# Two encoder-decoder layers and a rotary attention layer: the last layer's heads laid out in 64 rows by DMAs

## What is computed

```python
q = rope((x @ Wq).reshape(B, Sq, 16, 64)); k = rope((ctx @ Wk).reshape(B, Skv, 16, 64))
# rope: r1 = x1*cos - x2*sin, r2 = x2*cos + x1*sin, with x1 the even and x2 the odd columns of a head
scores = einsum('bqhd,bkhd->bhqk', q, k) / 8          # masked keys: -1e9
out = einsum('bhqk,bkhd->bqhd', softmax(scores), (ctx @ Wv).reshape(B, Skv, 16, 64))
y = layer_norm(x + out.reshape(B, Sq, 1024) @ Wo)
```

## Time and profile before

| | |
|---|---|
| median of 3 runs | 525.77 us (523.55 to 526.3) |
| the profiled execution | 527.22 us |
| its span, first to last instruction | 525.3 us |
| PE busy | 506.3 us, 96% |
| DVE, ACT, POOL busy | 436.8, 367.6, 295.5 us |
| mean granted TensorE clock | 0.992 |
| DMA, share of the 16 engines from the second tenth of the span on | 0 to 2 tenths |

### The profile page before, as it was taken

One profiled execution on the slowest core, in us unless ns is written; L12 is line 12 of the kernel. 1 busy time (PEld: TensorE's weight loads), 2 busy tenths in 40 slices (PEclk: granted clock), 3 DMA queues, 4 the chain that ended last, 5 costly groups with the idle time before them and its releaser, 6 DMA issues.

```text
span 525.3 us, 23789 instructions
## 1 busy us (share of the span) xinstructions
PE 506.3 (96%) x10336; PEld 470.6 (90%) x10336; DVE 436.8 (83%) x776; ACT 367.6 (70%) x1002; POOL 295.5 (56%) x581
## 2 busy tenths in 40 slices
PE   6989999999999999999999999999999999999986
PEld 6789999999999999999999998889999999999885
DVE  4898999977889877877878788999889888888873
ACT  5676675765876766767567686678687887888761
POOL 2553534534437445343536335888777887887825
PEclk9999999999999999999999999999999999999989
DMA  7910000000012010000000000000000000000000
GB/s 236 316 69 4 4 2 2 2 4 2 3 42 82 2 43 3 2 3 1 4 2 2 2 2 2 3 3 4 2 8 9 14 8 9 13 8 9 7 9 21
DMA packets 10838, 12.74 MB, mean 24 GB/s; under 512 B 752, under 2 KB 8432, under 8 KB 10736
## 3 DMA queue, kind: packets, MB, share of 16 engines
q1 hardware_dynamic: 10736, 11.24, 7.0%
HBM read 10.18 MB, written 1.05 MB: 21 GB/s over the span
## 4 chain that ended last, share of the span: by engine, by line
PE 78%; ACT 12%; DVE 4%; issue 2%; POOL 1%; DMA 1%; SPq 0%; POOLq 0%; DVEq 0%
PE ps_p L677 14%; PE ps_p L507 7%; PE ps_p L648 7%; PE ps_p L509 7%; PE ps_p L508 7%; ACT kT L762 6%; PE ps_a L562 5%; PE ps_a L584 5%; PE ps_p L637 4%; PE ps_a L544 4%; PE ps_p L639 4%; PE ps_p L638 4%; PE ps_p L584 4%; PE ps_p L698 2%; ACT probs L800 2%; PE ps_a L555 2%
## 5 line engine op out<-in xcount | busy, mean ns | idle before, releaser
L1179 POOL TENSOR_TENSOR small<-mv,epsilon 128x1 f32<-128x1 f32 x48 | 9.6, 199 | 170.1 <-DVE mv L936 170.1
L677 PE MATMUL ps_p<-wo,headsT 128*128 128x128 f32 x768 | 95.3, 278 | 2.0 <-DVE headsT L915 0.9
L677 PEld LDWEIGHTS ps_p<-wo,headsT 128*128 128x128 f32 x768 | 91.4, 193 | 5.2 <-issue 1.9
L907 DVE TENSOR_TENSOR turn<-ps_p,rope 128x1024 f32<-128x1024 f32 x64 | 76.0, 1221 | 11.6 <-PE ps_p L509 10.2
L754 ACT ACTIVATE vv<-ps_p 128x512 f32<-128x512 f32 x96 | 57.1, 619 | 27.3 <-PE ps_p L639 23.8
L507 PE MATMUL ps_p<-xT_hi,wq_hi 128*128 128x256 f32 x192 | 58.6, 305 | 1.1 <-issue 0.8
L790 ACT ACTIVATE probs<-ps_a,top 128x64 f32<-128x64 f32 x256 | 56.0, 353 | 4.4 <-DVE top L980 3.4
L1010 DVE TENSOR_REDUCE total<-probs 128x16 f32<-128x1024 f32 x48 | 58.2, 1212 | 0.2
L762 ACT ACTIVATE qT<-ps_p,columns 128x256 f32<-128x256 f32 x126 | 49.4, 494 | 10.1 <-PE ps_p L509 10.1
L508 PE MATMUL ps_p<-xT_lo,wq_hi 128*128 128x256 f32 x192 | 54.2, 282 | 0.0
L509 PE MATMUL ps_p<-xT_hi,wq_lo 128*128 128x256 f32 x192 | 54.1, 282 | 0.0
(11 more groups left out here) (143 smaller groups left out, 1429.2 us busy)
## 6 DMA issues: line engine op xcount, KB each, us to landing
out<-y_out SPq DMA_DIRECT2D x16, 64.0 KB, 2.8
X<-in_x SPq DMA_DIRECT2D x1, 768.0 KB, 7.6
across<-in_across SPq DMA_DIRECT2D x1, 704.0 KB, 9.5
wq_raw<-in_L_xattn_sa_wq SPq DMA_DIRECT2D x2, 256.0 KB, 2.9
wk_raw<-in_L_xattn_sa_wk SPq DMA_DIRECT2D x1, 512.0 KB, 5.9
wv_raw<-in_L_xattn_sa_wv SPq DMA_DIRECT2D x1, 512.0 KB, 8.2
wo<-in_L_xattn_sa_wo SPq DMA_DIRECT2D x1, 512.0 KB, 8.2
wo<-in_L_xattn_ca_wo SPq DMA_DIRECT2D x1, 512.0 KB, 8.7
```

The costliest lines, as they stand in the source:

```text
L677: last = mm(bank[:, 0:E], headsT[:, p, :, :].rearrange("r b q -> r (b q)"), wo[:, layer % 2, p, :], start=(p == 0), stop=(p == PAIRS - 1))
L907: ins = V.tensor_tensor(turn[:, j % 2, :, :].rearrange("d a (h b t) -> d a h b t", h=2, t=S), bank[:, None, :].broadcast_to([128, 2, 512]) ...
```

## The change

The weights of the last layer's queries and keys are put in another order of columns before the launch, so that a group of 128 rows holds the even or the odd columns of four heads. POOL no longer adds into `qT` and `kT` but into `w_raw[0]` (groups 0 and 1) and `w_raw[1]` (groups 2 and 3). When both groups of such a pair are there, SP issues 8 DMAs from SBUF to SBUF, each of 32 rows, two pieces of 1 KB a row, 64 KB, which put the even and the odd half of a head below each other in `qT` or `kT`: this is a move. There are four a chunk, 32 in all. A head then has 64 rows, and the last layer uses the scores, maxima and exponentials of the other layers, with two banks; `fold` and the split last addition go. PE waits, before the scores of an even unit, for all moves of its chunk. POOL waits, before it adds the first group of a pair, until the former move out of that buffer has landed. SP waits for the two additions, and for the scores of the chunk before last, which read the same half of `qT` and `kT`.

From step 36 on the keys come half a chunk ahead: step 36 has the four query groups and key groups 0 and 1; each odd step has key groups 2 and 3 of its chunk first and then 0 and 1 of the next chunk; step 45 has only groups 2 and 3. The number of groups over all steps stays. The rest of the diff renames `split_heads` to `scaled_queries` and takes out its branches.

```diff
@@ -64,6 +64,20 @@
+KEYS_AHEAD = 36
+def rotated_keys(u):
+    g = projected(u)
+    if u < KEYS_AHEAD:
+        return [(j, g) for j in range(4)] if u % 2 else []
+    if u % 2 == 0:
+        return [(0, g), (1, g)] if u == KEYS_AHEAD else []
+    return [(2, g), (3, g)] + ([(0, g + 1), (1, g + 1)] if g + 1 < N // 2 else [])
...
@@ -115,16 +129,17 @@
     project = []
-    if projected(u) is not None:
+    if rotary(u):
+        project = ([] if u % 2 else [("Qr", j, "D") for j in range(4)]) + [("Kr", j, "D") for j, _ in rotated_keys(u)]
+    elif projected(u) is not None:
         name = "K" if u % 2 else "Q"
-        for j in range(4):
-            project.append((name + "r", j, "D") if rotary(u) else (name, j, ("AAAD" if u == FIRST else "ADAD" if u < 0 else "AAAA")[j]))
+        project = [(name, j, ("AAAD" if u == FIRST else "ADAD" if u < 0 else "AAAA")[j]) for j in range(4)]
     next_in = [("T", 0, "AD")] if u % 2 and by_head(u + 1) else []
         into, inside, outof = ffn if ffn_chunk(u) is not None else ([], [], [])
-        return deferred + into + project[:2] + heads + project[2:] + values + inside + result + outof + probabilities + next_in
+        return deferred + into + project[:2] + heads + project[2:4] + values + project[4:] + inside + result + outof + probabilities + next_in
     if ffn_chunk(u) is not None:
...
@@ -200,12 +215,27 @@
-def rotations(name, j):
-    return (0, 1) if (name, j) == ("Kr", 3) else (1,)
-ROTATED = Tally(lambda u: [(n, j, v) for n, j, _ in fills(u) if n[1:] == "r" for v in rotations(n, j)])
+ROTATED = Tally(lambda u: [(n, j) for n, j, _ in fills(u) if n[1:] == "r"])
+def group_chunk(u, name, j):
+    return projected(u) if name == "Qr" else dict(rotated_keys(u))[j]
+MOVES = [(u, n, j // 2, group_chunk(u, n, j)) for u in range(FIRST, END) for n, j, _ in fills(u) if n[1:] == "r" and j % 2]
+def moves_ahead(u, name, place):
+    of = [m[:2] for m in MOVES if m[2] == place]
+    return of.index((u, name))
+def moves_for(g, place):
+    return max(k for k, m in enumerate(m for m in MOVES if m[2] == place) if m[3] == g) + 1
...
@@ -436,6 +466,11 @@
+        def apart(place):
+            return w_raw[place][:, :].rearrange("d (h j t) -> d h j t", h=2, j=2)
...
@@ -496,6 +531,17 @@
                     sp.dma_start(result[:, done % UNITS:done % UNITS + 1, :], y_out[:, v:v + 1, :]).then_inc(stored[v], 16)
+                for _, name, place, g in [m for m in MOVES if m[0] == u]:
+                    sp.wait_ge(rotated, ROTATED.at(u, name, 2 * place + 1))
+                    sp.wait_ge(scored, SCORED.at(2 * g - 3))
+                    to = (qT if name == "Qr" else kT)[:, g % 2, 4 * place:4 * place + 4, :]\
+                        .rearrange("r (j two) t -> r two j t", two=2)
+                    for i in range(4):
+                        for half in range(2):
+                            at = 64 * (i // 2) + 32 * half
+                            sp.dma_start(to[at:at + 32, i % 2, :, :], apart(place)[32 * i:32 * i + 32, half, :, :])\
+                              .then_inc(moved[place], 16)
             for v in range(2):
...
@@ -516,36 +562,12 @@
-                if layer == 2:
-                    pe.wait_ge(rotated, ROTATED.at(u - 1 - v, "Kr", 3, v))
+                if v == 0 and layer == 2:
+                    for place in range(2):
+                        pe.wait_ge(moved[place], MOVED * moves_for(u // 2, place))
                 elif v == 0:
                     out_of_bank(u - 1, "K", 3)
-                if layer == 2:
-                    if u == 2 * UNITS:
-                        pe.wait_ge(setup_dve, FOLD)
-                        pe.wait_ge(headed, HEADED.before(u))
-                    for i in range(4):
-                        for b in range(2):
-                            of = slice(32 * i, 32 * i + 32)
-                            m = mask[of, 1, u % UNITS, b:b + 1, :]
-                            mm(ps_a[64 * b:64 * b + 64, i ^ b, 0:256], fold[of, :], m.broadcast_to([32, 4, S]),
-                               start=True, stop=False, skip_group_check=True)
-                    for quad in range(H // 4):
-                        for half in range(2):
-                            for i in range(4):
-                                for b in range(2):
-                                    t = (2 * v + b) * S
-                                    of = slice(32 * i, 32 * i + 32)
-                                    last = mm(ps_a[64 * b:64 * b + 64, i ^ b, 64 * quad:64 * quad + 64],
-                                              qT[of, par, 2 * quad + half, t:t + S], kT[of, par, 2 * quad + half, t:t + S],
-                                              start=False, stop=half == 1, skip_group_check=True)
-                    last.then_inc(scored, 1)
-                    return
...
@@ -650,18 +672,20 @@
                     n_w = "QK".index(name[0])
-                    g = projected(u)
+                    g = group_chunk(u, name, j) if name[1:] == "r" else projected(u)
                     x = [s[:, :, 0:2 * S] for s in inputs_of(g)[n_w]]
                     if j == 0:
-                        pe.wait_ge(act_emptied, EMPTY_A.at(turn_in_step(g), "T", 0))
-                        pe.wait_ge(dve_emptied, EMPTY_D.at(turn_in_step(g), "T", 0))
+                        turning = turn_in_step(g - UNITS // CU if name == "Kr" else g)
+                        pe.wait_ge(act_emptied, EMPTY_A.at(turning, "T", 0))
+                        pe.wait_ge(dve_emptied, EMPTY_D.at(turning, "T", 0))
                         if g * CU % UNITS == 0:
-                        of = slice(256 * j + k, 256 * j + 256, 2) if name[1:] == "r" else slice(128 * (2 * j + k), 128 * (2 * j + k) + 128)
+                        of = slice(128 * (2 * j + k), 128 * (2 * j + k) + 128)
                         last = split_product(by_unit(bank[:, CT * k:CT * k + CT]),
...
@@ -879,10 +898,8 @@
-                    if j >= 2:
-                        dve.wait_ge(rotated, ROTATED.at(u, name, j - 2, 1))
-                    elif ROTATED.before(u):
-                        dve.wait_ge(rotated, ROTATED.at(u - 1, "Qr" if u % 2 else "Kr", j + 2, 1))
+                    if ROTATED.at(u, name, j) > 2:
+                        dve.wait_ge(rotated, ROTATED.at(u, name, j) - 2)
                 if name in ("T", "FT"):
...
@@ -1131,14 +1135,15 @@
             def rotate(u, groups):
-                for j in groups:
-                    name, to = ("Kr", kT) if u % 2 else ("Qr", qT)
+                for name, j in groups:
                     pool.wait_ge(dve_emptied, EMPTY_D.at(u, name, j))
-                    parts = rotations(name, j)
-                    for v in parts:
-                        of = slice(128 * v, 128 * v + 128) if len(parts) == 2 else slice(0, CT)
-                        G.tensor_tensor(to[:, projected(u) % 2, 2 * j:2 * j + 2, of], *[t[:, :, of] for t in turned(j)],
-                                        ALU.add).then_inc(rotated, 1)
+                    if j % 2 == 0:
+                        if moves_ahead(u, name, j // 2):
+                            pool.wait_ge(moved[j // 2], MOVED * moves_ahead(u, name, j // 2))
+                        else:
+                            pool.wait_ge(w_ready[j // 2], parts_ready(2, j // 2))
+                    G.tensor_tensor(apart(j // 2)[:, :, j % 2, :], *turned(j), ALU.add).then_inc(rotated, 1)
...
@@ -1297,6 +1303,10 @@
+    for n in "qk":
+        w = arrays["L1_xattn_W" + n].reshape(E, H // 4, 2, 2, D // 2, 2)
+        arrays["L1_xattn_W" + n] = np.ascontiguousarray(w.transpose(0, 1, 5, 3, 2, 4).reshape(E, H * D))
     aps = {name: nc.dram_tensor("in_" + name, v.shape, mybir.dt.from_np(v.dtype), kind="ExternalInput").ap()
```

More of the change, by code:

```diff
@@ L176, in vector_steps @@
         if name == "max":
-            steps += [("max", at)] + ([("eighth",)] if by_head(u) and not split_heads(u) and at else [])
+            steps += [("max", at)] + ([("eighth",)] if by_head(u) and not scaled_queries(u) and at else [])
         elif name == "sum":
-            steps += [("sum",), ("recip",)] + ([] if split_heads(u) else [("rinv",)])
+            steps += [("sum",), ("recip",)] + ([] if scaled_queries(u) else [("rinv",)])
         elif name == "fstat":
@@ L223, in vector_order @@
     before = [("norm", j, u - 1) for j in range(1 if rest_by_scalar(u - 1) else 2)] if by_head(u - 1) else []
-    maxima = [("max", 0)] + ([] if split_heads(u) else [("max", 1)])
+    maxima = [("max", 0)] + ([] if scaled_queries(u) else [("max", 1)])
     fgain = [("fgain", 0)] if gained(u) is not None else []
@@ L391, in build @@
         rotated = sem("rotated")
+        moved = [sem(f"moved{k}") for k in range(2)]
         stored = [sem(f"stored{v}") for v in range(2)]
@@ L775, in heads_out, with scale_of @@
                       .then_inc(headed, 1)
+            def scale_of(u):
+                return 1.0 if scaled_queries(u) else float(D) ** -0.5
             def exponentials(u, j):
```

(42 more changed lines are left out.)

24 lines of the change are left out of this document (9 added, 15 removed).

## The result

The changed kernel takes 602.86 us (median of 4 runs, 601.33 to 604.01), the kernel before 524.84 us beside it on the same chip: a ratio of 1.149 [1.145, 1.154], slower by 78 us. The sign of the forecast was right, its size was not: 561 us with a range of 537 to 580 was said. The profiled execution has a span of 599.9 us against 525.3.

What follows compares the result with a forecast made beforehand. The prediction took PE's work in the last layer as the bound. Terms of 10.1 + 6.8 + 18.8 + 0.3 = +36.0 us on the profiled 527.22 gave 563.2; with the median 1.45 lower it said 561 us, range 537 to 580.

Steps and rivals of the forecast that it cites:

- The failed step: SP's issues of a move: seven distances of 0.43 us, 3.0 in all, SP held 3.4 us, so it keeps up.
- the steady pair: Two steps from 38 to 46: 25.0 us instead of 20.29, +4.7 each, +18.8 for four pairs.
- M: Time of one move from POOL's last add to the data being there: 5.3 us, bounds 4.2 and 7.1.
- Steps 33 and 35: Odd steps before the order changes: keys' adds, then their move, make them later by 3.9 and 2.2 us.
- The ring of waits: Steps 36 to 46: POOL waits for buffer 1 until 17.0 us into a pair, DVE's turns for POOL, PE for turns.
- quick moves: Rival for all moves: 4.2 us each and the clock stays high, +10 us, 536 us; chance 0.17.
- The clock's eight times 1.2: PE's clock falls after each of eight waits at the even scores from 32 to 46, costing 1.2 us each.
- POOL's wait for the buffer: Steps 36 to 46: adds of Kr2 and Kr3 wait until the queries' move leaves buffer 1, at 17.0 us.
- The scores' gain: Last layer's scores with 64 rows: 1.17 us instead of 1.61, 0.44 less in 16 steps, 7.0 us in all.
- The rival that the gain does not exist: 64-row scores take 1.6 us, not 1.17: at most 7 us more; chance 0.03 with hidden moves, about 526.
- Slow moves: Rival for all moves: landing 3.6 us or more, 7.1 a move, full clock loss, 588 us; chance 0.13.
- Hidden moves: Rival from step 38 on: below 2.7 us a move nothing waits, the scores' gain shows, 518.8 us; chance 0.07.

Runs made afterwards that it cites:

- e3: The changed kernel with each move in 4 DMAs of 64 rows, 128 KB each, instead of 8 of 32 rows, same result: 543.91 us, 1.038.
- e6: The changed kernel with a separate tile for the keys' sums, still 8 DMAs a move: 591.15 us, 1.129.
- e1: The changed kernel with 64-row scores but no moves and keys never ahead, heads mixed: 519.55 us, 0.990 of the kernel before.
- e7: The changed kernel with extra unused PE products before the even scores' waits and some output projections, to hold the clock up: 603.8 us, 1.153.
- e4: The changed kernel with each move as one straight DMA of 512 KB, heads mixed: 526.51 us, 1.003 of the kernel before.
- e9: The changed kernel with 4 DMAs a move, keys half then a whole chunk ahead, and a separate tile for keys' sums, same result: 520.51 us, 0.9925.
- e11: e9 with 8 DMAs a move instead of 4, same result: 557.83 us, 1.065 of the kernel before.
- e10: The kernel before plus four trains of 8 DMAs of 64 KB on idle SP, from HBM or SBUF, 128 or 32 rows: 524.01 us in a single run.

## Why the prediction was wrong, step by step

**The failed step** is the term "I take 0.43 each, 3.0 us" with what was built on it: "occupies SP for 3.4. Two moves a step are 6.9 of 10 us, so SP keeps up". The distance of two issues came from loads out of HBM and single stores; from SBUF to SBUF it is 0.64 us, and up to 0.8 on average in a move that has a long issue. A move holds SP for 5.06 to 6.25 us. In the steady pair the four moves and two stores hold it for 22.7 us, where a pair had taken 20.29. One M comes to 7 times 0.64 + 2.0 + 0.1 = 6.6, inside its bounds of 4.2 to 7.1. The time that SP is held had been given no bounds. Below, the growth of the lateness at the scores (starts after, less those in the earlier trace rows and the 494.56 that the prediction gives).

| scores of | forecast | measured |
|---|---|---|
| 32 | +3.2 | 348.87 - 344.86 = +4.0 |
| 34 | +7.1 | 379.77 - 369.14 = +10.6 |
| 36 | +10.1 | 412.76 - 393.21 = +19.6 |
| 38 | +16.9 | 447.19 - 413.50 = +33.7 |
| 46 | +35.7 | 571.02 - 494.56 = +76.5 |
| end of the span | +36.0 | 599.9 - 525.3 = +74.6 |

**Steps 33 and 35.** The sum put the keys' last move behind the keys' adds alone. In the trace it stands behind three other moves in SP, and the adds themselves wait until the queries' move has left buffer 1. SP, POOL and PE of the changed kernel, steps 34 and 35, and the scores that follow:
```profile
388.86 5.06 SPq L543 DMA_DIRECT2D qT<-wq_raw  x8
394.01 5.98 SPq L543 DMA_DIRECT2D qT<-wk_raw  x8
400.04 0.58 SPq L533 DMA_DIRECT2D out<-y_out  x1
400.72 5.33 SPq L543 DMA_DIRECT2D kT<-wq_raw  x8
401.54 2.55 POOL L1146 TENSOR_TENSOR wk_raw<-turn 128x512 f32<-128x512 f32 x2 [1.73 <-DMA qT<-wk_raw]
406.15 5.07 SPq L543 DMA_DIRECT2D kT<-wk_raw  x8
...
412.76 0.64 PE L577 MATMUL ps_a<-mask,eye_bf 64*64 64x512 bf16 x4 [7.58 <-DMA kT<-wk_raw]
```
From 388.86 to 411.22 SP has no gap above 0.1 us. The adds end at 404.09, and their move waits 2.06 us more for SP. That is a neglected queue; by the starts of the adds in this trace it would not have shown with 3.4 us a move, an estimate of mine that no run tests.

**The steady pair.** Forecast 25.0, measured 30.83. The ring of waits was right: Q0 and Q1 ended at 8.6 in the pair (forecast 8.2). From there to buffer 1 being free it took 531.63 - 518.53 = 13.1 us (forecast 17.0 - 8.2 = 8.8), +4.3: the first move held SP for 5.9 in place of 3.5 with its wake-up (+2.4), and the second took 7.2 from its first issue to the free buffer in place of 5.3 (+1.9). From the end of the keys' adds to the scores it took 6.6 (forecast 5.3), +1.3. With +0.4 at the start that is 6.0, of 5.8 to be explained. Four such pairs grew by 123.83 - 81.06 = 42.8 us (forecast 18.8); that is 24.0 of the 38.6 us by which the span's growth was missed, another 16.8 had come by the scores of 38, and the end gave 2.2 back. e3, whose moves are about as long as "quick moves" had them (M near 4.1), measured 543.9, where that rival's sum said 536 with no clock loss. So the sum comes within 8 us when it is given its M. The clock's eight times 1.2 would bring it to 546, but in e3's trace the clock fell at only three of the eight scores and its mean was 0.990, so those 8 us are not explained by that.

**POOL's wait for the buffer** was foreseen (26 us in 6 waits), but its way back to PE was not counted as a stall of PE. e6 prices the sharing at 11 us.

**The scores' gain** was 0.44 a step and is 0.32: 5.1 in place of 7.0 us. The follower of the two rows was not the same. The rival that the gain does not exist falls by e1.

**The clock.** 1.2 us times eight stood in the sum. The clock did fall to 0.50 around the scores of all eight waits, as the trace before had shown once. In the steady pair it delays the turn of Q0 by 1.56 us against e7, and that turn is in the pair's chain, so the term was of the right kind and near in size. What it is worth in the whole kernel stays open: e7 held the clock up and took as long, for buffer 0 came free too late and SP's issues took longer. The Trainium skill (TensorE: Matmul & The Clock Gate, section HAM oscillation) says that the low clock comes back in each round of such a loop. The trace agrees, with 0.50 in each of the eight rounds; that its full price is then paid in each, 4 us more in the sum, no run here shows.

**The rivals.** "Slow moves" gave 588 and was nearest, but it made the landing slow (3.6) and left the issues fast; the landing was the term that I had nearly right. "Hidden moves" set 2.7 us as its point. e4 has about 2.9 + 0.1 = 3.0, and from 38 on its pairs take 19.74 us: next to that point the moves are hidden and the scores' gain shows, as the rival said, and only the steps before 38 bring the total back to 526.5. e9 moves the point itself by fetching earlier and is faster. Where the 78 us are: e9 against the change shows that three edits take them all away; by themselves, fewer issues are worth 59 (e3) and the buffer some 11 (e6), and with the buffer and the order mended, 8 issues against 4 still cost 37 (e11 against e9). Not tried: issuing part of the moves from another engine.

## What to carry to other kernels

Price a train of DMAs twice: once as a latency (distance of the issues times their number, and one landing) and once as time for which the queue's engine is held, and write that engine's instructions down in order before saying that it keeps up. Take the distance from issues with the same kinds of source and destination, and if no row has them, give the distance bounds that also go into the queue's sum. A slow clock behind a wait can lie in the chain and still give nothing back when it is mended, if a buffer or a queue comes right behind it (e7); look for that one before adding the clock's price.

## What the runs showed of the hardware that was not expected

- An issue on SP took 0.59 to 0.60 us from SBUF to SBUF and 0.42 to 0.43 from HBM, with the same bytes and rows (e10). More bytes did not make an issue longer: 64 KB 0.597, 128 KB 0.607, 512 KB in a single DMA 0.465. Why SBUF to SBUF is dearer is open. That the source lies in SBUF isn't enough, since a y_out store takes 0.33 when alone, and 0.58 right behind a train of moves.
- The queries' moves held SP for 5.81 and 5.63 us in the steady pair and the keys' for 5.06 each, with the same shapes. The difference is single long issues, 14 of the 256, of up to 1.71 us. All 14 overlap in time with a packet of 16 KB that the trace calls "instruction", and no such packet that runs while a move is being issued meets normal issues only. In the ten kernels with moves, 115 of the 116 issues of over 0.8 us overlap with such a packet. That the fetching of code makes the issue long is likely, but no run removed it. The page's row for these packets (number, MB, share of the 16 DMA engines):
```profile
q8 instruction: 74, 1.21, 0.8%
```
- The Trainium skill (DMA: Bandwidth & Descriptors, section Issuing engines are not separate DMA queues) calls a sequencer's issue time usually small beside the DMA. For a train of DMAs this case's trace disagrees: a single issue is 0.60 us against a landing of 2.0, but eight issues took 5.06 us one after the other, and the last landing ended 2.0 us after its issue had begun.
